# A cross-interaction tower on one core: the fourth unit of every first-layer group is multiplied in plain fp32 on TensorE, behind the first unit, in place of being split in two by ScalarE and GpSimd

## The reference

```python
x_vec = input                                    # input = e, the looked-up rows
for W, b in [(W0, b0), (W1, b1), (W2, b2)]:      # 128 outputs each
    z = jnp.einsum('bhd,bfd->bhfd', x_vec, input)
    x_vec = jnp.einsum('oc,bcd->bod', W, z.reshape(B, h * f, d)) + b[None, :, None]
    outs.append(x_vec.sum(axis=2))
h = jnp.concatenate([jnp.concatenate(outs, axis=1), dense_ctx], axis=1)
h = jnp.maximum(h @ W_top1 + b_top1, 0.0)
h = jnp.maximum(h @ W_top2 + b_top2, 0.0)
y = h @ W_top3
```

## Time and profile before

| | |
|---|---|
| median of 3 runs | 1192.84 us (1191.19 to 1193.23) |
| the profiled execution's own time | 1193.48 us |
| its span | 1191.7 us |
| granted TensorE clock over the span | 0.996 of full speed |
| busy share | PE 94%, PEld 64%, DVE 85%, POOL 83%, ACT 59% |
| mean busy share of the DMA engines, from the queues' shares | about 41% |

### The profile page before, as it was taken

One profiled execution on the slowest core, in us unless ns is written; L12 is line 12 of the kernel. 1 busy time (PEld: TensorE's weight loads), 2 busy tenths in 40 slices (PEclk: granted clock), 3 DMA queues, 4 the chain that ended last, 5 costly groups with the idle time before them and its releaser, 6 DMA issues.

```text
span 1191.7 us, 13969 instructions
## 1 busy us (share of the span) xinstructions
PE 1120.7 (94%) x4212; PEld 758.3 (64%) x4212; DVE 1011.0 (85%) x685; ACT 704.5 (59%) x682; POOL 989.1 (83%) x419
## 2 busy tenths in 40 slices
PE   0379999999999999999999999999999999999998
PEld 0146666666666666666766666666666666667685
DVE  4478998989989999989898998999898889897542
ACT  2245566566666666675666666656666666665533
POOL 6669999999999999999999999999999997776000
PEclk9989999999999999999999999999999999999999
DMA  6552232525252515334252524252342525242991
GB/s 226 137 161 65 85 83 78 161 65 166 73 150 63 155 46 147 91 88 150 64 165 73 156 78 133 68 144 71 111 127 76 154 73 160 76 151 106 273 297 48
DMA packets 103835, 142.85 MB, mean 120 GB/s; under 512 B 11745, under 2 KB 55009, under 8 KB 103042
## 3 DMA queue, kind: packets, MB, share of 16 engines
q1 hardware_dynamic: 95618, 140.42, 39.1%
q0 software_dynamic: 8192, 2.11, 2.0%
HBM read 114.96 MB, written 27.53 MB: 120 GB/s over the span
## 4 chain that ended last, share of the span: by engine, by line
POOL 62%; PE 17%; issue 14%; DMA 4%; DVE 1%; SPq 1%; ACT 1%; POOLq 0%; ACTq 0%; DVEq 0%
POOL z_lo L509 46%; POOL emb L500 16%; PE acc L1015 9%; PE acc L1010 3%; DMA z<-gram_scratch 3%; PE turn_gram_ps L1079 1%; DMA land<-x_scratch 1%; PE z_ps L1141 1%; ACT z_hi L977 0%; DVE z_lo L754 0%; DVE z L577 0%; SPq L441 0%; SPq L369 0%; PE x0t_ps L1183 0%; PE turn_gram_ps L1183 0%
## 5 line engine op out<-in xcount | busy, mean ns | idle before, releaser
L509 POOL TENSOR_TENSOR z_lo<-z,z_hi 128x2048 fp32r<-128x2048 f32 x159 | 734.9, 4622 | 47.0 <-ACT z_hi L789 44.1
L1015 PE MATMUL acc<-z_hi,w_hi 128*128 128x512 f32 x960 | 412.4, 430 | 3.0 <-POOL z_lo L509 2.1
L789 ACT ACTIVATE z_hi<-z 128x2048 fp32r<-128x2048 f32 x160 | 306.3, 1914 | 181.4 <-PE acc L1015 170.4
L1015 PE MATMUL acc<-z_hi,w_lo 128*128 128x512 f32 x960 | 378.8, 395 | 0.0
L1015 PE MATMUL acc<-z_lo,w_hi 128*128 128x512 f32 x960 | 378.8, 395 | 0.0
L577 DVE TENSOR_TENSOR z<-operand_even,x_shift 128x2048 f32<-128x2048 f32 x144 | 328.5, 2282 | 31.8 <-DMA x_shift<-x_scratch 16.8
L500 POOL DMA_INDIRECT emb<-in_tables,rows_chunk x256 | 254.0, 992 | 62.0 <-issue 56.9
L1010 PE MATMUL acc<-z,w_sb 128*128 128x512 f32 x640 | 293.7, 602 | 0.6 <-ACT x L818 0.4
L589 DVE TENSOR_TENSOR z_lo<-z_ps,z_hi 128x1024 fp32r<-128x1024 f32 x160 | 194.5, 1215 | 71.0 <-ACT z_hi L798 71.0
L1015 PEld LDWEIGHTS acc<-z_hi,w_hi 128*128 128x128 f32 x960 | 180.8, 188 | 62.8 <-issue 18.9
L577 DVE TENSOR_TENSOR z<-operand_odd,x_shift 128x2048 f32<-128x2048 f32 x96 | 218.8, 2279 | 0.5 <-ACT operand_odd L765 0.3
(11 more groups left out here) (92 smaller groups left out, 454.2 us busy)
## 6 DMA issues: line engine op xcount, KB each, us to landing
land<-x_scratch SPq DMA_DIRECT2D x128, 256.0 KB
land<-x_scratch SPq DMA_DIRECT2D x128, 128.0 KB
x_shift<-x_scratch SPq DMA_DIRECT2D x16, 1024.0 KB, 5.8
gram_scratch<-gram SPq DMA_DIRECT2D x32, 512.0 KB, 4.3
x_shift<-x_scratch SPq DMA_DIRECT2D x16, 768.0 KB, 7.7
z<-gram_scratch SPq DMA_DIRECT2D x10, 1024.0 KB, 10.8
x_scratch<-emb SPq DMA_DIRECT2D x32, 192.0 KB, 2.9
x_shift<-gram_scratch SPq DMA_DIRECT2D x6, 1024.0 KB, 10.5
```

The costliest lines, as they stand in the source:

```text
L509: pool.tensor_tensor(z_lo[:, slot], z[:, Z_SLOT[pos]], z_hi[:, slot].bitcast(F32), ALU.subtract).then_inc(subtracted, 1)
L789: act.activation(z_hi[:, SPLIT_SLOT[pos]], z[:, Z_SLOT[pos]], ACT.Copy).then_inc(rounded, 1)
L1015: mm = pe.matmul(acc[:, :], w[:, tile, :], zz[:, slot, q, :], start=False, stop=stop and n == 2)
```

## The change

What becomes of position 3 of each of the 16 layer-1 groups (m3 above):

- ACT no longer rounds it and POOL no longer subtracts it. PE multiplies it as a plain unit, right behind position 0. The order of a layer-1 group on PE is then 0, 3, 1, 2 in place of 0, 1, 2, 3; layer 2 keeps its order.
- The waits follow the new order. DVE may form d3 when m3 has been used; ACT may round d1 when three units of m are used, in place of two; it may round d3 without a wait.
- The weights of that position are kept as plain fp32 (four more plain tiles, four fewer split ones in each of `w_hi` and `w_lo`).
- POOL's look-ups keep their places: those that stood behind m3's low part now stand behind m1's. The first two rounds of POOL come out of its loop. The low part of chunk 0's position 3 goes.
- The last part of the third layer's weights is loaded two units later, because a weight tile that it overwrites is in use for longer.

```diff
-L1_SPLIT = SPLIT_UNITS * QUAD
+L1_SPLIT = 2 * QUAD
-L1_PLAIN, L2_PLAIN = QUAD, L2_GROUPS * QUAD
+L1_PLAIN, L2_PLAIN = 2 * QUAD, L2_GROUPS * QUAD
...
-            load_w2(3, 3)
+            load_w2(3, 3, units_used=2)
...
                     for pos in (1, 3):
-                        low_part(Group(c, j), pos)
+                        if not (pos == 3 and Group(c, j).is_layer1):
+                            low_part(Group(c, j), pos)
                         if look_up and done == 0:
                             begin_gathers(c.plus(2))
...
-            low_part(layer1_group(Chunk(0, 0)), 3)
-            with pool.Fori(0, (CHUNKS - 2) // 2) as n:
-                round_(Chunk(n, 0))
-                round_(Chunk(n, 1))
+            round_(Chunk(0, 0))
+            round_(Chunk(0, 1))
+            with pool.Fori(0, (CHUNKS - 4) // 2) as n:
+                round_(Chunk(n, 2))
+                round_(Chunk(n, 3))
...
                     if pos == 0:
                         dve.wait_ge(used, g.count(4, -3))
+                    elif pos == 3 and g.after_layer1:
+                        dve.wait_ge(used, g.count(4, -2))
                     else:
-                        dve.wait_ge(subtracted, g.count(2, -2 + (pos + 1) // 2))
+                        dve.wait_ge(subtracted, g.units(-1 if pos == 1 and not g.after_layer1 else 0))
...
                 if not g.is_first:
-                    act.wait_ge(used, g.count(4, pos - 3))
+                    if pos == 1:
+                        act.wait_ge(used, g.count(4, -1 if g.after_layer1 else -2))
+                    elif not g.after_layer1:
+                        act.wait_ge(used, g.count(4))
                 act.activation(z_hi[:, SPLIT_SLOT[pos]], z[:, Z_SLOT[pos]], ACT.Copy).then_inc(rounded, 1)
...
-                        act.wait_ge(used, g.count(4, -1))
+                        act.wait_ge(used, g.count(4, 0 if g.after_layer1 else -1))
...
-                round_unit(m, 3)
...
                 float_unit(g, acc1, w0_sb, 0)
+                float_unit(g, acc1, w0_sb, QUAD, pos=3)
                 split_unit(g, 1, acc1, 0)
-                halves_unit(g, acc1, QUAD)
-                split_unit(g, 3, acc1, 2 * QUAD, stop=True)
+                halves_unit(g, acc1, QUAD, stop=True)
```

More of the change, by code:

```diff
@@ L121, in __init__, with units @@
         self.is_first = chunk.is_(0) and j == -1
+        self.last_chunk = chunk.is_(CHUNKS - 1)
+        if chunk.is_(0):
+            self.is_layer1, self.after_layer1 = j < 1, j in (0, 1)
+        else:
+            self.is_layer1, self.after_layer1 = (not self.last_chunk and j == n for n in (2, 3))
     def count(self, per_group, more=0):
         return self.chunk.count(GROUPS * per_group, per_group * (1 + self.j) + more)
+    def units(self, more=0):
+        if self.chunk.is_(0):
+            return 2 * (1 + self.j) - min(1 + self.j, 2) + more
+        return self.chunk.count(2 * GROUPS - 1, 2 * (1 + self.j) - 1 - (self.j > 2 and not self.last_chunk) + more)
     def copies(self, more=0):
@@ L453, in reload_gram, with load_w2 @@
                 load_gram(k)
-            def load_w2(part, groups_used):
-                sp.wait_ge(used, Group(end, groups_used).count(4))
+            def load_w2(part, groups_used, units_used=0):
+                sp.wait_ge(used, Group(end, groups_used).count(4, units_used))
                 sp.dma_start(w2_parts[part], w2[:, part * W2_PART:(part + 1) * W2_PART, :]).then_inc(w2_in[part], 16)
@@ L507, in low_part @@
                 slot = SPLIT_SLOT[pos]
-                pool.wait_ge(rounded, g.count(2, (pos + 1) // 2))
+                pool.wait_ge(rounded, g.units((pos + 1) // 2))
                 pool.tensor_tensor(z_lo[:, slot], z[:, Z_SLOT[pos]], z_hi[:, slot].bitcast(F32),
@@ L900, in _ @@
             round_half(g0, 0)
-            round_unit(g0, 3)
             round_half(g0, 1)
@@ L913, in _ @@
             round_half(g1, 0)
-            round_unit(g1, 3)
             round_half(g1, 1)
@@ L1005, in _, with float_unit @@
         def _(pe):
-            def float_unit(g, acc, weights, tile0, start=False):
-                pe.wait_ge(formed, g.count(3, 2))
+            def float_unit(g, acc, weights, tile0, pos=0, start=False):
+                pe.wait_ge(formed, g.count(3, 2 if pos == 0 else 3))
                 for q in range(QUAD):
-                    mm = pe.matmul(acc[:, :], weights[:, tile0 + q, :], z[:, Z_SLOT[0], q, :], start=start and q == 0, stop=False)
+                    mm = pe.matmul(acc[:, :], weights[:, tile0 + q, :], z[:, Z_SLOT[pos], q, :], start=start and q == 0, stop=False)
                 mm.then_inc(used, 1)
@@ L1018, in split_unit @@
             def split_unit(g, pos, acc, tile0, stop=False):
-                pe.wait_ge(subtracted, g.count(2, (pos + 1) // 2))
+                pe.wait_ge(subtracted, g.units((pos + 1) // 2))
                 for q in range(QUAD):
@@ L1023, in split_unit, with halves_unit @@
                 mm.then_inc(used, 1)
-            def halves_unit(g, acc, tile0):
+            def halves_unit(g, acc, tile0, stop=False):
                 for half, done in enumerate((half_used, used)):
@@ L1029, in halves_unit @@
                     for q in (2 * half, 2 * half + 1):
-                        mm = split_tile(acc, tile0 + q, SPLIT_SLOT[2], q, False)
+                        mm = split_tile(acc, tile0 + q, SPLIT_SLOT[2], q, stop and q == QUAD - 1)
                     mm.then_inc(done, 1)
@@ L1234 @@
         "ids": ids, "field_info": info, "tables": np.concatenate(table_list, axis=0), "dense": a["dense_ctx"].T,
-        "w0a": np.concatenate([pairs[:, :, 1].reshape(P, -1), squares], axis=1).reshape(P, L1_PLAIN + 1, HID),
-        "w0b": np.concatenate([pairs_turned[:, :, 1].reshape(P, -1), np.zeros_like(squares)], axis=1),
-        "w0a_split": pairs[:, :, [0, 2, 3]].reshape(P, L1_SPLIT, HID), "w0b_split": pairs_turned[:, :, [0, 2, 3]].reshape(P, L1_SPLIT, HID),
+        "w0a": np.concatenate([pairs[:, :, [1, 3]].reshape(P, -1), squares], axis=1).reshape(P, L1_PLAIN + 1, HID),
+        "w0b": np.concatenate([pairs_turned[:, :, [1, 3]].reshape(P, -1), np.zeros_like(squares)], axis=1),
+        "w0a_split": pairs[:, :, [0, 2]].reshape(P, L1_SPLIT, HID), "w0b_split": pairs_turned[:, :, [0, 2]].reshape(P, L1_SPLIT, HID),
         "w1": w1[:, :, 0].reshape(P, L2_PLAIN, HID), "w1_split": w1[:, :, 1:].reshape(P, L2_SPLIT, HID), "w2": w2,
```

## The result

The changed kernel takes 1230.19 us (median of 4 runs, 1227.22 to 1231.87), against 1192.77 us before: a ratio of 1.0313, with a 95% interval of 1.0294 to 1.0332. The forecast was 1231.3 us. The span of the profiled execution grew from 1191.7 to 1228.4 us, 36.7 us more.

What follows compares the result with a forecast made beforehand. POOL was taken to bound the kernel, 65.12 us a round; after the change a dependence loop of 67.91 us would. Rounds +34.8, start +3.0, end +0.65: +38.4 us, giving 1231.3 us, range 1210 to 1243.

Steps and rivals of the forecast that it cites:

- What bounds the kernel now: Before the change, POOL sets the round at 65.12 us, above PE's 64.73 and a dependence loop of 64.47.
- the DMA leg: From POOL's last look-up of a round to ACT's copy of m's first row pair: mean 16.14 us.
- PE: A plain unit takes 3.44 us against 2.79 split: +0.65 us a round, making PE's own round 65.38 us.
- POOL's idle time: POOL, its look-ups behind m1 done early, sits idle some 6 us until ACT rounds d1.
- The order on PE: Plain m3 stands between m0 and m1, so m1 is used 3.44 us later; m3 is ready in time.
- The loop: Dependences through all engines once a round grow from 64.47 to 67.91 us: +34.8 us over 13 rounds; chance 0.75.
- The two waits of PE: Each round PE waits about 1.1 us before d3 and about 1 us before the gram needing DVE's block 0.
- only d3: Rival: the reload is hidden, only PE's wait before d3 remains: 66.4 us a round, 1211 us; chance 0.07.
- The start: Behind chunk 1's layer-1 group, ACT's rounding of the next position 1 waits 3.44 us longer: +3.0 us.
- The end: Behind the last layer-1 group POOL has no look-ups and PE's own time holds: +0.65 us; later third-layer weights cost nothing.
- PE alone: Rival: the loop has overlooked slack, only PE's work of 65.38 us a round stays: 1195 us; chance 0.09.
- POOL's relief: Rival: POOL was the bound, so each round loses 4.62 us: 1133 us; chance 0.05, or a part of it.

Runs made afterwards that it cites:

- both moved: Changed kernel with no look-ups between d1 and d3 on POOL and the round's last look-up before e3 instead of behind it: 1199.56 us, ratio 1.0052.
- dve_low: Kernel before, with DVE instead of POOL making m3's low part: 1193.62 us, ratio 0.9999.
- dve_low_looks: Kernel before, DVE making m3's low part, look-ups moved: none between d1 and d3, the last before e3: 1188.91 us, ratio 0.9962.
- dve_low_pair: Kernel before, DVE making m3's low part, SP fetching m's first row pair before the shifted copies: 1187.18 us, ratio 0.9937.

## Why the prediction was right

**What bounds the kernel now.** POOL at 65.12 us, PE at 64.73 and a loop at 64.47 were the right three. The word "bounds" was half right for POOL: with POOL relieved by DVE the round fell by 0.1 us only, since the low part on DVE lengthened the loop to some 64.95 us. The step from there to the 65.14 that was measured is argued, not tried: the DMA leg was 0.09 us longer on average (16.23 us), and it varies (15.44 to 17.16 us in the kernel before), and a round takes the longest of its terms, so the mean of the rounds can lie above the longest of the means. One reading was wrong and its number right: between the layer-1 groups of chunks 14 and 15, POOL still had look-ups, the last at 983.63 us, so that row alone did not show PE's own round. The three runs with PE free of waits do, at 64.73.

**PE.** +0.65 us a round was forecast; 65.36 against 64.73 is 0.63.

**POOL's idle time.** "Some 6 us" before d1 was 6.3 to 8.1 us. The prediction's own terms, 67.91 - 60.5, give 7.4; it had no part in the sum.

**The order on PE.** The step on which all rests: m1 used 3.44 us later. In the trace the leg from the gram to d1's rounding went from 17.01 to 20.44 us, +3.43, and turning the order took 35 us back.

**The loop.** 67.91 was forecast and 67.76 measured; the legs stand above, each within 0.12 us. 13 rounds were to give +34.8 and gave +32.9 us. The DMA leg was sized well (a mean of 16.11 us over the 13 rounds, for 16.14); the term a little too large is the last leg, from d1's rounding to the end of d3's low part, 13.54 us for 13.66. The median came within 1.1 us of the forecast, nearer than the 1.9 us by which the rounds were oversized and well inside the 4.6 us over which the runs spread: so near a hit is partly luck.

**The two waits of PE.** "About 1.1 us before d3" was recorded as 0.98, but costs 1.4 us (66.74 against 65.36). I set PE's work of 12.67 us against 13.66, wrote 1.1 and used the difference, 1.0. The starts of PE's matmuls say where the rest is. With the last look-up moved, against both moved: 1.24 us lie between d0 and e0, and 0.12 in group e, at e3. The 1.24 are the recorded wait, 0.16 by which the record of the matmul before it (0.39 us) outlasts the 0.23 us from one start to the next, and 0.10 because the next start follows in 0.33 us and not 0.23. The wait had no part in the sum, but in a rival: "only d3" should have been 1216, not 1211 us, and that is where two runs that left only this wait came out.

**The start.** +3.0 was forecast and +3.1 measured at the group of chunk 2, on the path that was named:

```profile
87.47 1.92 ACT L807 ACTIVATE z_hi<-z 128x2048 fp32r<-128x2048 f32 x1 [7.45 <-PE acc L1030]
...
89.47 4.54 POOL L520 TENSOR_TENSOR z_lo<-z,z_hi 128x2048 fp32r<-128x2048 f32 x1 [7.85 <-ACT z_hi L807]
```

ACT rounds at 87.47 in place of 83.61 and POOL begins at 89.47 in place of 86.09. Both are 0.42 us later than forecast (87.05 and 89.05), of which the group of chunk 2 shows 0.1.

**The end.** +0.65 forecast, +0.7 measured. The later third-layer weights cost nothing that can be seen.

**The rivals.** PE alone would have been 1195 us. It is the right price for the right kernel: with the order turned it was 1195.6. POOL's relief as a gain of 4.6 us a round fell with the runs in which DVE took the low part: PE's 64.73 us is a floor. By the Trainium skill's rule on the most-contended engine ("Perfetto Trace Analysis", Identifying the Most-Contended Engine) PE, with weight loads at 64%, should have had room (the section names the use of peak FLOPs beside them, which was not worked out here); here its matmuls stood end to end at that figure, and the measurement decides.

## What to carry to other kernels

When several engines are nearly full, look for a path that goes once round all of them in each iteration (a buffer released, a unit made, a look-up issued behind it in the same queue, a reload, a first use) and add up its legs. Work taken off a full engine is worth nothing if the edit lengthens that path, and so it is if the engine that takes the work over stands in the path too. Swapping two units in one engine's list can be worth more than the work itself. Put what a long transfer depends on early in its queue, and put a unit early if its buffer is waited for.

## What the runs showed of the hardware that was not expected

Where DVE makes a low part, both its operands lie in SBUF; in its forming and its other low parts one lies in PSUM. Timelines of the run in which DVE makes m3's low part, DVE and then POOL:

```profile
625.79 2.28 DVE L654 TENSOR_TENSOR z_lo<-z,z_hi 128x2048 fp32r<-128x2048 f32 x1
```

```profile
625.62 0.94 POOL L500 DMA_INDIRECT emb<-in_tables,rows_chunk  x1 [0.30 <-issue]
626.87 2.02 POOL L500 DMA_INDIRECT emb<-in_tables,rows_chunk  x1 [0.30 <-issue]
```

The look-up that began 1.08 us into DVE's instruction took 2.02 us in place of 0.94, and ended at 628.89, 0.8 us after DVE's instruction did. So it is in all 39 rounds of the runs dve_low, dve_low_looks and dve_low_pair: a look-up that began while DVE's low part ran took 1.9 to 2.9 us and ended 0.81 to 0.83 us after it. The look-up before it, which had begun before DVE's instruction (0.17 us before, in these rows), took its usual time, and so did DVE, 2.28 us.

The Trainium skill ("SBUF — State Buffer", SBUF: two separate sides) says that GpSimd and VectorE share a port pair, that whichever starts first has it for its whole instruction, and that a VectorE instruction with two SBUF inputs asks for it only against a GpSimd operation that reads SBUF. The look-ups that began second agree with this. The ones that began first do not show it: they ran on for up to 0.9 us beside DVE's instruction, and neither was the longer for it. What of a look-up needs the port, the rows do not tell. It costs nothing here, since POOL waits behind it anyway (3.5 us before d1 in that round).
